# Attention kernel: the second quarter of the first step's keys loaded during the middle stage over dead tokens, the masks in the front, the last two stores in the attention

## The reference, cut to what matters

```python
xn = _layernorm(x)
x = x + L0_attn(xn) + L0_ffn(xn)          # recurrence over 2048 tokens; sign weights
xn = _layernorm(x)
x = x + L1_attn(xn) + L1_ffn(xn)
# L1_attn: causal softmax attention, 16 heads of 16, with ALiBi slopes
scores = einsum('bhqd,bhkd->bhqk', Q, K) / sqrt(hd) + slopes * rel
attn = softmax(where(rel <= 0, scores, -inf))
# L1_ffn: rmsnorm, causal attention (16 heads on 4 key heads, rotary), then 8 experts, 2 per token
```

## Time and profile before

| | |
|---|---|
| median of 3 timed runs | 2362.65 us (2357.61 to 2364.03) |
| profiled execution, its own time | 2358.44 us |
| span of its trace | 2356.0 us |
| PE busy over the span | 92% |
| DVE busy over the span | 86% |
| mean granted clock of PE | 0.956 of full speed |
| middle stage ends, attention begins | 325.5 us |
| first score product of the attention | 350.1 us |

### The profile page before, as it was taken

The page is one execution under the profiler, slowest core; times in us unless marked ns, Lnnn a source line. Parts: engine busy times, 40 slices in busy tenths (PEclk is TensorE's granted clock), DMA queues, the critical chain, the costliest instruction groups (busy, mean ns, idle before and its releaser), DMA issues. The chain is left out here.

```text
span 2356.0 us, 47793 instructions
## 1 busy us (share of the span) xinstructions
PE 2176.4 (92%) x15828; PEld 1282.4 (54%) x15829; DVE 2028.9 (86%) x5148; ACT 1542.3 (65%) x2993; POOL 671.4 (28%) x997
## 2 busy tenths in 40 slices
PE   4599968999999999999999999999998894999997
PEld 2355544444444444444444544544543783888886
DVE  7799858999999999999999999999991664777775
ACT  3144414678888888888888888888888452444443
POOL 5523002232322322322322322322211254333333
PEclk8799977999999999999999999999999886999999
DMA  5179875654554654432432432433222895444443
GB/s 169 58 217 266 276 179 77 119 118 90 103 107 88 108 107 86 92 84 63 92 85 63 92 78 70 92 76 72 69 89 64 292 307 215 78 81 81 82 81 70
DMA packets 176412, 273.23 MB, mean 116 GB/s; under 512 B 53608, under 2 KB 126072, under 8 KB 170372
## 3 DMA queue, kind: packets, MB, share of 16 engines
q0 software_dynamic: 45840, 137.55, 28.6%
q1 hardware_dynamic: 125332, 122.86, 17.3%
q10 hardware_dynamic: 5044, 10.32, 1.5%
HBM read 128.64 MB, written 140.98 MB: 114 GB/s over the span
## 5 line engine op out<-in xcount | busy, mean ns | idle before, releaser
L1524 ACT ACTIVATE a_p<-banks 128x512 f32<-128x512 f32 x2176 | 1131.2, 608 | 256.8 <-PE banks L1417 206.8
L1577 DVE TENSOR_REDUCE a_mx<-banks 128x1 f32<-128x512 f32 x1536 | 943.4, 680 | 20.1 <-PE banks L1406 20.0
L1485 PE MATMUL banks<-a_p,a_v 128*32 128x512 f32 (+3 forms) x5120 | 589.0, 544 | 1.6 <-ACT a_o L1542 1.1
L1406 PE MATMUL banks<-a_k,a_q 52*128 52x512 f32 (+5 forms) x1600 | 446.8, 413 | 1.9 <-DVE a_rowtop L1574 0.3
L1417 PE MATMUL banks<-a_q,a_k 50*128 50x512 f32 (+7 forms) x1600 | 415.8, 396 | 1.1
L1574 DVE CUSTOM_DVE_ANT_0 a_masked<-banks,a_later 128x512 bf16<-128x512 f32 (+3 forms) x768 | 330.8, 484 | 19.2 <-PE banks L1406 17.3
L1417 PEld LDWEIGHTS banks<-a_q,a_k 54*128 54x128 f32 (+1 forms) x1600 | 227.3, 185 | 198.7 <-DVE a_mx L1577 95.6
L1406 PEld LDWEIGHTS banks<-a_k,a_q 52*128 52x128 f32 (+1 forms) x1600 | 224.1, 185 | 118.0 <-DVE a_mx L1577 55.4
L1406 PE MATMUL banks<-a_k,q 48*128 48x512 f32 (+6 forms) x896 | 256.7, 420 | 6.2 <-DMA a_k<-aug_rows 4.6
L1417 PE MATMUL banks<-q,a_k 50*128 50x512 f32 (+7 forms) x896 | 231.5, 402 | 1.1 <-DVE a_orow L1597 0.3
L1485 PEld LDWEIGHTS banks<-a_p,a_v 128*32 128x32 f32 x5120 | 109.3, 108 | 175.0 <-issue 125.3
(11 more groups left out here) (276 smaller groups left out, 2997.2 us busy)
## 6 DMA issues: line engine op xcount, KB each, us to landing
expert_rows<-a_zeros POOLq DMA_DIRECT2D x132, 258.0 KB, 5.3
a_k<-ka_parts POOLq DMA_DIRECT2D x42, 256.0 KB, 6.3
e_x<-expert_rows SPq DMA_DIRECT2D x71, 129.0 KB, 2.3
expert_rows<-e_y SPq DMA_DIRECT2D x71, 128.0 KB
qa_parts<-m_part SPq DMA_DIRECT2D x16, 512.0 KB
ka_parts<-m_part SPq DMA_DIRECT2D x16, 512.0 KB
va_tiles<-m_va SPq DMA_DIRECT2D x8, 1024.0 KB, 6.8
qb_parts<-m_part SPq DMA_DIRECT2D x16, 512.0 KB, 3.8
```

The lines of the kernel that those rows point to most:

```text
L1406: ins = pe.matmul(ps[bank][:, col:col + w], q_op[r % 3][part, p, qt * P:(qt + 1) * P], keys_of(r, k0)[part, kp, k0:k0 + w], start=True, st ...
L1485: ins = pe.matmul(ps_o[VW * h:VW * h + VW, c0:c0 + w], v_op[o][:, kt, hk * VW:hk * VW + VW], prob[:, (at + slot) % NPB, col:col + w], star ...
L1524: nc.scalar.activation(prob[:, (t * NSC + n) % NPB, :], ps[bank][:, :], ACT.Exp, scale=SCALE).then_inc(s_ex, 1)
L1577: ins = v.tensor_reduce(top, ps[bank][:, :], AX.X, ALU.max)
```

## The change

- The mask `later` (256 KB) and the token numbers `numbers` (16 KB) are loaded in the front, by SP, and counted by `s_masks`; all waits on it are now for 5 x 16. Before, SP loaded `later` and POOL loaded `numbers` at the start of the attention.
- The first step's key tile is now at a fixed place over sequence 0's half of `xnT`. In the middle POOL loads keys 0 to 1023 into it (`EARLY`), not keys 0 to 511 into `k0a`. POOL's wait in block 5 covers the stores m = 0 to 3, not only 0 and 1.
- SP loads keys 1024 to 1535 at the start of the attention, ACT keys 1536 to 2047. `KEYED` follows.
- Block 7's last two stores (`kb` and `vb`) are issued by SP in the attention behind its key loads, and nobody waits at the end of the middle for the stores of parts and values. POOL waits for all of them before its first load of step 1.
- The `keep_going` at the end of the middle has 36 products instead of 20; the one of 10 before the first r is gone.

```diff
@@ front, sync @@
-            for dst, src in ((M["fill"], "c_fill"),
+            for dst, src in ((M["fill"], "c_fill"), (M["later"], "c_later"), (M["numbers"], "c_ids"),
                              (M["after_q"][0], "c_after0"), (M["after_q"][1], "c_after1")):
@@ first_keys @@
+EARLY = 2 * BT
-        eng.dma_start(M["k0a"][at:at + HD, :, :].bitcast(F32),
-                      M["ka_d"][PROD_K[n], 0:GH * HD, 0:BT].rearrange("(p j d) t -> j d p t", p=PAIRS, j=2)[j]
+        eng.dma_start(M["k0"][at:at + HD, :, 0:EARLY].bitcast(F32),
+                      M["ka_d"][PROD_K[n], 0:GH * HD, 0:EARLY].rearrange("(p j d) t -> j d p t", p=PAIRS, j=2)[j]
...
+def first_keys_at(nc, M):
+    at = SBUF_START + F32_BYTES * (P + WIDE + TOK // P + PAIRS * L) + BF16_BYTES * (HALF + 2 * P)
+    M["k0"] = nc.alloc_sbuf_tensor_at("k0", [P, PAIRS, L], F32R, offset=at)
...
+def last_stores(eng, M):
+    eng.dma_start(M["kb_d"][:, (B - 1) * P:B * P, L - BT:L].rearrange("a f t -> f a t"),
+                  M["last_part"][:, :, :].bitcast(F32)).then_inc(M["s_moved"][NBLK - 2], 16)
+    eng.dma_start(M["vb_d"].rearrange("(n p) c -> p n c", p=P)[:, TOK // P - TPB:TOK // P, :],
+                  M["last_values"][:, :, :, :].rearrange("p j h c -> p j (h c)")).then_inc(M["s_moved"][NBLK - 1], 16)
@@ middle, gpsimd @@
-                    for m in range(2):
+                    for m in range(4):
                         pool.wait_ge(s_pst[m], NBB * 16 + 16)
@@ middle, sync @@
                     sp.wait_ge(s_lo, blk * NS + (m + 1))
+                    if blk == NBLK - 1 and m == NS - 1:
+                        break
...
-            for m in range(NS):
-                sp.wait_ge(s_pst[m], NBLK * 16 + 16)
...
-            sp.wait_ge(s_vst, NBLK * 32 + 16)
@@ middle, tensor @@
-            keep_going(pe, M, ps[0], 20)
+            keep_going(pe, M, ps[0], 36)
@@ attention @@
-KEYED = [min(m for m in range(NMX) if MAXES[m][2][0][2] >= k0) for k0 in (WIDE, 2 * WIDE)]
+KEYED = [min(m for m in range(NMX) if MAXES[m][2][0][2] >= k0) for k0 in (EARLY, EARLY + BT)]
...
-            sp.dma_start(later[:, :], A["c_later"]).then_inc(M["s_masks"], 16)
-            first_step_keys(sp, s_k[0], BT, 2 * BT)
+            first_step_keys(sp, s_k[0], EARLY, EARLY + BT)
+            last_stores(sp, M)
...
+                        if n // 5 == 4:
+                            for done, count in zip(M["s_moved"], M["moved"]):
+                                pool.wait_ge(done, count)
...
-            pe.wait_ge(M["s_masks"], 64)
+            pe.wait_ge(M["s_masks"], NMASKS)
...
-                        if t == 0 and n == 0:
-                            keep_going(pe, M, ps_o, 10)
...
-            first_step_keys(act, s_k[1], 2 * BT, L)
+            first_step_keys(act, s_k[1], EARLY + BT, L)
```

More of the change, by code:

```diff
@@ L13 @@
 ds = bass.ds
+SBUF_START, SBUF_END = 16512, 229344
+F32_BYTES, BF16_BYTES = 4, 2
 P = 128
@@ L514, in middle @@
         vb_d = M["vb_d"].rearrange("(n p) c -> p n c", p=P)
+        M["last_part"], M["last_values"] = part[NS - 1], vb
         NW = 10
@@ L1105, in attention @@
         ps, ident = M["ps"], M["ident"]
-        q_op = [M["q0"], *(sb(f"a_q{i}", [P, PAIRS, L], F32R) for i in range(1, 3))]
+        sb("a_room_k0", [P, PAIRS, L], F32R)
+        q1 = sb("a_q1", [P, PAIRS, L], F32R)
         v_op = [sb(f"a_v{i}", [P, KT, GH * VW]) for i in range(3)]
@@ L1109, in attention @@
         fill, after_q = M["fill"], M["after_q"]
-        later = sb("a_later", [P, WIDE])
+        later, numbers = M["later"], M["numbers"]
         masked = sb("a_masked", [P, 2, WIDE], BF16)
@@ L1119, in attention @@
         zeros = sb("a_zeros", [P, FILL, DR])
-        numbers = sb("a_numbers", [P, TOK // P])
         raw_w = sb("a_raww", [P, WIDE], F32R)
         high_w = sb("a_highw", [P, WIDE], F32R)
-        k_op = [sb(f"a_k{i}", [P, PAIRS, L], F32R) for i in (0, 2, 1)]
-        k_op = [k_op[0], k_op[2], k_op[1]]
+        q_op = [M["q0"], q1, sb("a_q2", [P, PAIRS, L], F32R)]
+        k2, k1 = sb("a_k2", [P, PAIRS, L], F32R), sb("a_k1", [P, PAIRS, L], F32R)
+        k_op = [M["k0"], k1, k2]
         ps_o = ps[RING]
@@ L1156, in attention @@
         DIRECT = 2
+        NMASKS = 5 * 16
         TOPS = NQB - DIRECT
@@ L1292, in _ @@
             nc.gpsimd.memset(zeros[:, :, :], 0.0).then_inc(s_hi, 1)
-            pool.dma_start(numbers[:, :], A["c_ids"]).then_inc(s_zs, 16)
             pool.wait_ge(s_hi, 1)
-            pool.wait_ge(s_zs, 16)
+            pool.wait_ge(M["s_masks"], NMASKS)
             nc.gpsimd.tensor_copy(zeros[:, :, D], numbers[:, 0:1].to_broadcast([P, FILL])).then_inc(s_hi, 1)
@@ L1386, in mask @@
                 return ins
-            def keys_of(r, k0):
-                return M["k0a"] if r == 0 and k0 < BT else k_op[r % 3]
             holder = {}
@@ L1406, in max_half @@
                     ins = pe.matmul(ps[bank][:, col:col + w], q_op[r % 3][part, p, qt * P:(qt + 1) * P],
-                                    keys_of(r, k0)[part, kp, k0:k0 + w], start=True, stop=True)
+                                    k_op[r % 3][part, kp, k0:k0 + w], start=True, stop=True)
                 ins.then_inc(s_mt, 1)
@@ L1416, in score_half @@
                     kp = 0 if r >= NGB else p
-                    ins = pe.matmul(ps[bank][:, col:col + w], keys_of(r, kt * P)[part, kp, kt * P:(kt + 1) * P],
+                    ins = pe.matmul(ps[bank][:, col:col + w], k_op[r % 3][part, kp, kt * P:(kt + 1) * P],
                                     q_op[r % 3][part, p, qb * QB + c0:qb * QB + c0 + w],
@@ L1603, in _ @@
                 step(t)
-SBUF_END = 229344
-F32_BYTES = 4
 def at_top(nc, M):
@@ L2397, in of_both @@
                 return early.enter_context(nc.sbuf_tensor(name, shape, dt))
-            M["k0a"] = of_both("k0a", [P, PAIRS, BT], F32R)
+            M["later"] = of_both("later", [P, WIDE], F32)
+            M["numbers"] = of_both("numbers", [P, TOK // P], F32)
             M["q0"] = of_both("q0", [P, PAIRS, L], F32R)
```

14 lines of the change are left out of this document (8 added, 6 removed).

## The result

| | before | changed |
|---|---|---|
| median (6 runs each) | 2363.34 us | 2349.74 us (2343.51 to 2352.85) |
| ratio of times, 95% interval | | 0.9945 [0.9935, 0.9955] |
| profiled execution, its own time | 2358.44 us | 2343.51 us |
| span of its trace | 2356.0 us | 2341.6 us |
| first score product | 350.08 us | 335.01 us |

The change is faster by 13.6 us in the medians and by 14.4 us in the spans; forecast were 2346 us and a gain of 14.4. That the spans give 14.4 to the digit is luck: a second execution of the changed kernel has a span of 2347.5 us. Most of the forecast's 3.7 us distance to the median lies in its base: it started from a mean of 2360.7, and the runs of the kernel before had by then a median of 2363.34.

The account below looks back on a forecast made before the run. A chain of waits where the middle meets the attention bounds, neither PE nor DVE. First scores 14.8 us earlier, less 0.4 in the middle, gain 14.4; from the mean of 2360.7 that gives 2346 us, range 2341 to 2351.

Parts of the forecast that it names:

- The chain of the seam: From the middle's end to the attention's first scores: a chain of waits bounds; first scores 14.8 us before 350.08.
- End of the middle: Middle's last block: PE's 36 products end it at 322.0, not SP; attention starts at 322.4 instead of 325.55, 3.1 us.
- DVE's first maximum: Start of the attention: 0.98 us behind PE's first product, at 323.4.
- Ten items at DVE's pace: Start of the attention: ten items of maxima take DVE 6.58 us, until 330.0; a full clock changes nothing.
- The turn: PE's turn of the maxima before ACT's copy: 0.5 us, until 331.2, with PE there in time.
- The transfer of the rows: Rows sent by SP at 331.8 behind the stores: landing between 334.6 and 336, taken as 335.3.
- The first rival: Row transfer waits for the whole backlog: scores start near 341, 8.7 us gained, 2352 us; chance 0.18.
- The middle: Doubled key loads delay block 4's `vb`; DVE stalls at the next values, 0.4 us taken, ends 0 and 2.7.
- The clock: PE's granted clock at the attention's start: near 1.00 up to 332.
- The second rival: Clock stays full behind the first scores: up to 1.3 us more per stretch, gain 17, 2344 us; chance 0.10.
- The third rival: Gain partly given back, by 2.7 us in the middle or a step 0 transfer: gain 7 to 12, 2351; chance 0.10.
- The slower rival: Granted clock stays at half in the attention: 80 us of it would give 2386 us; chance 0.03.

Follow-up runs that it names:

- e2_stores_back: Changed kernel with the last two stores issued in the middle again and all stores awaited at its end: median 2353.99 us, ratio 0.9957 against the kernel before.
- e4_keys_back: Changed kernel with only keys 0 to 511 loaded in the middle, 512 to 1023 at the attention's start: median 2354.57 us, ratio 0.9966 against the kernel before.
- e6_idle10_back: Changed kernel with the 10 idle products before the first turn of maxima put back: median 2352.88 us, ratio 0.9954 against the kernel before.

## Why the prediction was right

**The chain of the seam** held link by link but for the turn. Times from the first idle product, forecast (313.60 there) and measured (312.79 there):

| | forecast | measured |
|---|---|---|
| PE's first product of the attention | 8.8 | 9.01 |
| DVE's first maximum | 9.8 | 9.67 |
| maxima of the first 512 queries done | 16.4 | 16.25 |
| POOL's parts ready | 17.1 | 16.99 |
| ACT's copy starts | 17.6 | 18.19 |
| rows sent | 18.2 | 18.80 |
| first scores | 21.7 | 22.22 |

- **End of the middle.** That PE's products end the block and SP waits 2.1 us for them was right: 2.1 in the changed kernel, 0.2 with 20 products.
- **DVE's first maximum** stood 0.66 us behind PE's first product, 0.98 forecast: PE ran it at a clock of 1.00, and the row it was read from at 0.50.
- **Ten items at DVE's pace.** 6.58 us forecast and measured (322.46 to 329.04), although the clock was not the one expected. They take 6.58 or 6.59 us in all fourteen traces, with the clock at 0.50 all the way as with it at 1.00 for the first 4.6 us.
- **The turn** was the link mis-sized: 0.5 us forecast, 1.20 measured (329.78 to 330.98). The 0.5 came from a turn right behind idle products, at full clock. At half clock the four products take 1.01 us in place of 0.60, which is 0.4 of the 0.7. The rest is that they start 0.15 us behind POOL's parts, at 329.93, and that the 0.5 was counted from the end of the idle products at 346.24, while the turn had begun at 346.08.
- **The transfer of the rows** behind the stores: 3.5 us forecast, 3.42 measured, against 2.75 in the earlier trace rows. With the stores behind the rows it took 2.90 and, with 20 idle products, 2.75 in place of 4.12. So the two stores ahead cost 0.5 to 0.7 us in the changed kernel and 1.4 with 20 products. The first rival, a wait for the whole backlog until 341, is out: it priced keys in SP's queue at 0.327 us a packet, as in ACT's queue before. From 322 to 326 the packets of the changed kernel took 0.483 x 64 / 224 = 0.138 us in SP's queue and 0.467 x 64 / 200 = 0.149 in ACT's:

```profile
q1 hardware_dynamic: 224, 0.32, 48.3%
q10 hardware_dynamic: 200, 0.28, 46.7%
```

That the size came out was partly luck, for the model behind it isn't borne out. It had SP's queue busy with the stores until 334.3 to 335.2 and the rows landing then. The `vb` store in the changed kernel, and the same store in the one with 20 products (size, us to landing):

```profile
vb_tiles<-m_vb SPq DMA_DIRECT2D x1, 256.0 KB, 7.8
```

```profile
vb_tiles<-m_vb SPq DMA_DIRECT2D x1, 256.0 KB, 7.4
```

It landed at 333.0 in the first (325.24 + 7.8) and at 331.6 in the second (324.18 + 7.4), and PE began the scores 2.0 and 3.1 us later. So stores ahead make the rows late, but not just by their data, and why 4.12 us with 20 products, where the rows follow the stores at the same distance (6.35 us behind the issue of `vb`), stays open. By the Trainium skill (DMA: Bandwidth & Descriptors, section Queues, rings and completion order) one queue's ring is consumed in order; the runs agree as far as they show it, 3.42 and 4.12 us with stores ahead in the queue, 2.75 to 2.90 without.

DVE was not the limit that it might have been: it was through with the maxima at hand at 334.93 and then waited 1.63 us for PE, until 336.56.

**The middle.** The stall that the prediction placed at the values of block 5, 0.4 us, is not in this trace. The changed kernel at that place, the store of block 4's `vb` and DVE's rows behind it:

```profile
249.66 0.80 SPq L635 DMA_DIRECT2D vb_tiles<-m_vb  x1
...
259.08 1.40 DVE L965 TENSOR_TENSOR m_va<-banks,m_bv 128x256 f32<-128x256 f32 x4
...
261.74 0.69 DVE L942 TENSOR_TENSOR m_xf<-banks,m_cos 128x512 f32<-128x512 f32 x1 [0.93 <-PE banks L685]
```

And the same store in the DMA view, its size and us to landing:

```profile
vb_tiles<-m_vb SPq DMA_DIRECT2D x1, 256.0 KB, 8.4
```

SP issued the store 1.8 us earlier than before, at 249.66 for 251.48 (why, no run isolates), it landed at 258.1, and DVE's write came at 259.08 without a wait for it. DVE's wait for PE at 261.74 is 0.93, as before. But the margin is thin. In the eleven traces with the change's middle this store took 6.1 to 9.9 us, 7.8 in the mean, against 7.1 and 6.8 in the two with the middle of before. In the one with 9.9 (e2_stores_back) DVE did wait for it:

```profile
260.75 1.42 DVE L965 TENSOR_TENSOR m_va<-banks,m_bv 128x256 f32<-128x256 f32 x4 [0.44 <-DMA vb_tiles<-m_vb]
262.88 0.69 DVE L942 TENSOR_TENSOR m_xf<-banks,m_cos 128x512 f32<-128x512 f32 x1 [0.40 <-PE banks L685]
```

That is the stall of the forecast, and DVE's wait for PE behind it, 0.40 in place of 0.93, took it up, as the forecast said of most of it. How much of the store's length is the double key load isn't shown: 1.7 to 2.7 us more were expected, the means are 0.9 apart, and with half of the early keys one trace has 4.9 (e4_keys_back). POOL's wait for the `ka` stores moved its first query loads from 211.02 to 212.83, and its next wait shrank from 10.64 to 7.68 us: covered, as argued. The first idle product stands at 313.69 in the mean of the ten traces with the change's middle and such products (312.79 to 314.82), and at 313.60 and 313.19 in the two with the middle of before, so some tenths elsewhere can't be excluded.

**The clock** step failed, at little cost to the sum: it cost 0.4 us in the turn and gave 0.3 at DVE's first maximum. The prediction expected a clock near 1.00 up to 332; it was 0.50 from 325 on. The second rival (the clock stays full, gain 17) fell with it. The 16 extra products did put the fall off: it came 10.8 to 14.3 us behind K in the seven traces with 36 products and 7.3 to 8.6 in the six with 20. But what ran at full clock for that were, at best, the ten items at DVE's pace, which take 6.58 us either way. So they bought nothing: with 36 or 20 of them the ratios are 0.9945 and 0.9943, and with the stores behind the rows 0.9941, 0.9934 and, with none, 0.9941.

**From the seam to the end** the forecast took the gain at the first scores as the gain of the kernel. It was 15.07 us there in the two traces, of which 0.81 is only that K stands earlier in the changed one; 13.95 at the fifth parts, 13.69 when the attention ends (1820.40 and 1806.71, the start of the next stage) and 14.4 in the span. About 1 us was given back in step 0, inside the forecast's range of 2341 to 2351, but no more than the 1.4 us by which the same kernel differs from itself there; in the repeat the four gains are 14.8, 12.3, 12.1 and 8.5. So the sum came out with small errors of both signs: the chain gained 14.26 from K to S where 14.8 were forecast, the middle lost none of the 0.4, and what followed took back what one trace can't tell, with 13.6 in the medians. The third rival had this direction but not the size, and its two reasons (the middle, a transfer of step 0) were not what the trace showed. The slower rival is out: the part from 500 to 600 us runs at 1.00.

**What each part is worth.** At S, undone alone: stores 3.7, masks 2.7, early keys 4.0, the ten idle products 3.1 us, together 13.5 against the 14.3 of all. That the sum comes so close is partly chance; until the rows are sent it is 4.3, 3.4, 4.6 and 3.8, together 16.1. They are links of one chain, but not independent ones: whichever is undone, the rows then travel in 2.75 or 2.76 us in place of 3.42, since the stores are through by then, and a load put back moves the loads behind it. By the ratios they are worth 2.8, 2.1, 5.0 and 2.6 us of time, the same order of size; only that of the keys stands out of the scatter, and it just barely.

**What stays open.** The length of step 0 behind S runs from 124.07 to 131.27 us over the kernels, and is longer mostly where the granted clock is lower. The two ends, before and e4_keys_back, from S on:

```profile
350.08:474.08 124.00, 111.40 (x696) 55.51 (x696) 108.25 (x285) 66.86 (x126) 30.59 (x56) 0.82 0.55 93
```

```profile
339.72:463.72 124.00, 111.56 (x653) 56.86 (x653) 101.68 (x267) 61.61 (x117) 29.54 (x54) 0.73 0.54 88
```

PE is busy just as long in both but gets through 43 fewer products. The link is loose, though: at a clock of 0.78 the length was 125.54, 125.86 and 129.71. The masks undone had 0.81 and 124.78, one repaired transfer 0.72 and 129.85, and the same kernel twice differed by 1.4 us. Chance has a part in the clock: of 16 executions of the kernel before in one group of runs, the three shortest (2359.68 to 2360.37 us) had a mean clock of 0.954 over the span and the three longest (2366.93 to 2367.98) one of 0.950 and 0.951. Whether an edit at the seam has a part too in where the clock falls in step 0, one trace for each kernel doesn't say. It is worth up to 7 us, half of what the change gained.

## What to carry to other kernels

Where all engines are idle by turns, write the chain from one fixed event to the next as a list of links with a row for each, and move the loads and waits that stand in it; single parts then have a price that can be checked one by one. Here every link came within 0.4 us of its forecast but the turn, which was 0.7 off. A small transfer on which everybody waits landed sooner ahead of bulk stores of the same queue than behind them, and behind them it hides part of the gain of whatever makes it start earlier. Idle products meant to hold the clock must be priced like work: ten of them in the chain cost 3.1 us of it and sixteen more at the block's end 2.1 us of waiting. They did raise the clock or put off its fall, but of work that DVE or a transfer paced, and no run showed them giving it back.

## What the runs showed of the hardware that was not expected

- The granted clock was 0.94 in the stretch from 320 to 325, in which PE was busy 3.69 of 5.00 us, and 0.50 in the next, in which PE was busy 5.00 of 5.00 with products that DVE paces. 8.26 us of products without a pause just before did not hold it. In the repeat of the same kernel the two stretches have 1.00 and 0.60, so the place of the fall moves by 1 to 2 us by itself.
- PE's turn of the maxima took 0.60 us for its four products at a clock of 1.00 and 1.01 at 0.50, and one record of an idle product 0.22 us in the 20 at 331.25 (4.39 / 20, in e6_idle10_back), at a clock of 0.50 for the most part, but 0.115 in the 72 at 312.79 (8.26 / 72), at 1.00.
- In the middle one and the same store of 256 KB took 6.1 to 9.9 us in eleven traces whose instructions in the middle up to it do not differ, and only at 9.9 was an engine late by it, 0.44 us.
